# Masked cross attention: the transposing of the row maxima, the projections and the values moved later in the order of steps

## What is computed

```python
q = einsum('oc,bct->bot', Wq, target) + bq      # 256 x 512 for each batch
k = einsum('oc,bcs->bos', Wk, source) + bk
v = einsum('oc,bcs->bos', Wv, source) + bv      # all three: 16 heads of 16 rows
dot = einsum('bhdt,bhds->bhts', q, k) / 4
mask = target_mask[..., None] * source_mask[..., None, :]
dot = mask * dot - (1 - mask) * 1e6
out = einsum('bhts,bhds->bhdt', softmax(dot) * mask, v)
```

## Time and profile before

| what | value |
|---|---|
| median of 3 runs | 3598.25 us |
| the profiled execution | 3600.92 us |
| its span, first to last instruction | 3599.1 us |
| PE busy | 3035.9 us (84%) |
| DVE busy | 1701.8 us (47%) |
| ACT busy | 1241.4 us (34%) |
| POOL busy | 601.1 us (17%) |
| masked cross attention | from 464 us to about 1110 us |

### The profile page before, as it was taken

The page is one execution under the profiler, slowest core; times in us unless marked ns, Lnnn a source line. Parts: engine busy times, 40 slices in busy tenths (PEclk is TensorE's granted clock), DMA queues, the critical chain, the costliest instruction groups (busy, mean ns, idle before and its releaser), DMA issues. The chain is left out here.

```text
span 3599.1 us, 48594 instructions
## 1 busy us (share of the span) xinstructions
PE 3035.9 (84%) x16338; PEld 2037.3 (57%) x16339; DVE 1701.8 (47%) x3232; ACT 1241.4 (34%) x3220; POOL 601.1 (17%) x647
## 2 busy tenths in 40 slices
PE   6999849888881999999788885999999996999894
PEld 4676513333321777777545554888888885444441
DVE  5666646777752111112166663666666664111113
ACT  2333306555660111111044432655655552111110
POOL 1000031232233000000000001333333332300002
PEclk9999959989985999999899997999999998999997
DMA  1000057656734000000100002111211106201323
GB/s 64 19 23 23 13 127 142 147 121 155 142 83 144 12 13 12 13 13 18 44 13 23 23 18 77 48 48 58 83 59 48 41 30 239 108 0 35 128 93 114
DMA packets 127374, 235.40 MB, mean 65 GB/s; under 512 B 15384, under 2 KB 27928, under 8 KB 127216
## 3 DMA queue, kind: packets, MB, share of 16 engines
q1 hardware_dynamic: 106560, 190.20, 18.8%
q0 software_dynamic: 12528, 32.40, 2.7%
q10 hardware_dynamic: 8128, 10.67, 1.0%
HBM read 161.55 MB, written 71.14 MB: 65 GB/s over the span
## 5 line engine op out<-in xcount | busy, mean ns | idle before, releaser
L1295 DVE TENSOR_REDUCE x_minus_max<-banks 128x2 f32<-128x1024 f32 x256 | 308.5, 1223 | 176.4 <-PE banks L1361 174.9
L1243 ACT ACTIVATE x_probs<-banks 128x512 f32<-128x512 f32 x512 | 272.3, 598 | 135.2 <-PE banks L1379 127.5
L481 ACT ACTIVATE a_probs<-banks,a_minus_max 128x128 f32<-128x128 f32 (+1 forms) x512 | 208.6, 425 | 146.5 <-DVE a_minus_max L564 144.8
L1361 PE MATMUL banks<-x_stacked_k,x_stacked_q 51*128 51x512 f32 x512 | 135.6, 480 | 60.4 <-DVE x_whole L1312 21.2
L1379 PE MATMUL banks<-x_stacked_q,x_stacked_k 53*128 53x512 f32 x512 | 162.4, 534 | 22.2 <-ACT x_probs L1243 18.8
L1379 PEld LDWEIGHTS banks<-x_stacked_q,x_stacked_k 53*128 53x128 f32 x512 | 64.6, 203 | 204.4 <-issue 157.5
L2116 POOL TENSOR_TENSOR x_probs<-x_probs,x_inverse 128x512 f32<-128x512 f32 x128 | 133.1, 1040 | 274.6 <-DVE x_inverse L2325 274.6
L2850 DVE TENSOR_TENSOR m_h<-banks,m_silu 128x512 f32<-128x512 f32 x39 | 27.0, 692 | 318.8 <-PE banks L2966 166.3
L2180 ACT ACTIVATE x_probs<-banks,x_minus_max,x_rroot 128x256 f32<-128x256 f32 x256 | 142.9, 566 | 91.4 <-DVE x_minus_max L2291 91.4
L564 DVE TENSOR_REDUCE a_minus_max<-banks 128x2 f32<-128x512 f32 (+1 forms) x192 | 131.8, 687 | 82.4 <-PE banks L714 62.1
L1688 DVE TENSOR_TENSOR f_hT<-banks,f_silu 128x256 f32<-128x256 f32 (+1 forms) x88 | 37.3, 424 | 280.7 <-ACT f_silu L1614 280.7
(11 more groups left out here) (372 smaller groups left out, 7764.6 us busy)
## 6 DMA issues: line engine op xcount, KB each, us to landing
x_parts_dram<-x_parts SPq DMA_DIRECT2D x16, 1024.0 KB, 6.1
x_x<-x_after SPq DMA_DIRECT2D x24, 512.0 KB, 4.3
x_stacked_k<-x_parts_dram SPq DMA_DIRECT2D x96, 128.0 KB
x_stacked_q<-x_parts_dram SPq DMA_DIRECT2D x96, 128.0 KB
x_after<-a_z SPq DMA_DIRECT2D x16, 512.0 KB, 2.8
x_z<-x_after SPq DMA_DIRECT2D x16, 512.0 KB, 7.3
x_heads_dram<-x_heads_out SPq DMA_DIRECT2D x32, 256.0 KB, 4.6
x_after<-x_z SPq DMA_DIRECT2D x16, 512.0 KB, 3.7
```

Of the source, the lines that this page charges most:

```text
L481: ins = act.activation(probs[:, n % 3, i * width:(i + 1) * width], psum[uses.bank(use)][:, i * width:(i + 1) * width], ACT.Exp, bias=minus ...
L1243: act.activation(probs[:, n % 8, :], psum[at.bank(f"exp{n}")], ACT.Exp, scale=SCALE)\
L1295: dve.tensor_reduce(minus_max[:, c % 2, h % 4:h % 4 + 2, t], at.pair(use), AX.X, ALU.max, negate=True)\
```

## The change

`shift` moves from q = 15, 31, 47 and 63 to q = 18, 34, 50 and 66. ACT's copy of its rows is a step of its own now, `copy`, which stands at the same q. `maxima` stays. The projections move from q = 34, 38, 42 and 51 to q = 36, 40, 44 and 53, with their `whole` and `round`, and the second half of the values from q = 19 to q = 23. The first half stays at q = 6. No instruction is added or taken away.

```diff
--- before.py
+++ after.py
@@ -803,10 +803,11 @@
 UNIT_LEAD = 36
 UNITS_IN_TAIL = 1
 MAXIMA_AT = 12
-SHIFT_AT = 15
+SHIFT_AT = 18
+COPY_AT = 18
 SLOTS = 4 * 16
-PIECES_AT = (34, 38, 42, 51)
-VALUES_AT = (6, 19)
+PIECES_AT = (36, 40, 44, 53)
+VALUES_AT = (6, 23)
 FOLD = 32
 HALF = 64
 STACKED_PAIRS = ((0, 0), (0, 1), (1, 0))
@@ -848,7 +849,7 @@
             for kind, at in (("values'", 0), ("more'", 0), ("bias'", 2), ("mask'", 3)):
                 if q == start + at:
                     add((kind, n))
-        for kind, at in (("maxima", MAXIMA_AT), ("shift", SHIFT_AT)):
+        for kind, at in (("maxima", MAXIMA_AT), ("shift", SHIFT_AT), ("copy", COPY_AT)):
             if q in (at, at + 16):
                 add((kind, (q - at) // 16 + 2))
             if q in (at + 32, at + 48):
@@ -1242,10 +1243,9 @@
                         at.wait_full(act, f"exp{n}")
                         act.activation(probs[:, n % 8, :], psum[at.bank(f"exp{n}")], ACT.Exp, scale=SCALE)\
                             .then_inc(free[at.bank(f"exp{n}")], 1)
-                    if kind in ("shift", "shift'"):
-
-                        to = u if kind == "shift" else 1 - u
-                        use = f"{kind}{n}"
+                    if kind in ("copy", "copy'"):
+
+                        use = f"shift{n}" if kind == "copy" else f"shift'{n}"
                         at.wait_full(act, use)
                         act.copy(max_rows[:, n % 2, :], psum[at.bank(use)][0:8, :]).then_inc(free[at.bank(use)], 1)
                         at.wait_free(act, use)
```

## The result

| | before | after |
|---|---|---|
| median | 3599.18 us (3590.18 to 3605.63, 5 runs) | 3617.68 us (3614.4 to 3626.74, 5 runs) |
| the profiled execution | 3600.92 us | 3614.93 us |
| its span | 3599.1 us | 3613.1 us |
| PE's first row of the part that follows | 1120.1 us | 1133.1 us |

The ratio is 1.0051, with a 95% interval of 1.0033 to 1.007: slower, and inside the range. (The median before takes in two runs more than the 3598.25 us of the first table.) Of the 14.0 us between the profiled executions, 13.0 have come by the end of the masked cross attention. On ACT and POOL a line number is now one higher than before (L1244 for L1243, L1175 for L1174).

What follows compares the result with a forecast made beforehand. PE was taken to set the pace, the other engines mostly waiting for it. The terms 23.8 - 20.6 + 3.0 - 9.0 - 5.9 - 3.6 + 3.5 + 21.6 gave +12.8 us, 3611 us against the median of 3598.25; range 3586 to 3634.

Steps and rivals of the forecast that it cites:

- point 6: Later values, ACT's copy, SP's transfers, DMAs of shift 0 and 1: all have slack, so 0.
- point 7: Clock among the new waits of 1.54 us: two falls per batch at 1.8 us, six batches, +21.6 us.
- point 1: Projections two steps later: no context between the two scores, wait 1.54 for 0.55, cycle 6.05 for 5.06, +23.8 us.
- Point 2: Transposing three steps later: five long waits go, -20.6 us; cast still held, so third projection's `whole` late, +3.0 us.
- Point 4: Seam: last transposing and the score behind wait less, -5.9 us; two clock falls fewer, -3.6 us.
- point 3: Clock behind the stall: five falls of 1.8 us go with it, -9.0 us.
- point 5: Transposing at q = 50 takes a bank's turn; score at q = 52 waits some 0.7 in five batches, +3.5 us.
- The fourth rival: Wait moves to `exp 48`, for slower DMAs behind POOL's combine: 1 to 2 us in five batches, about 3618; chance 0.05.
- the pair in the earlier trace: Two PE waits of 0.50 and 0.81 within 2 us, followed by the lower clock; taken as nearest to 1.54.
- the third rival: Clock stays down among waits of 1.54 us: up to 78 us and 3667, half of that 3628; chance 0.10.

Runs made afterwards that it cites:

- run 3: Changed kernel with the projections at q = 38, 42, 46, 55 in place of 36, 40, 44, 53: 3606.69 us, ratio 1.0024 to the kernel before.
- run 4: Changed kernel with `whole` one step behind its projection in place of two: 3593.93 us, ratio 0.9988 to the kernel before.
- run 6: Kernel before with POOL's low parts moved behind the DMAs of the third shift: 3596.36 us, ratio 0.9992.
- run 12: Kernel before with only POOL's DMAs of shift 3 moved ahead of the combine: 3574.37 us, ratio 0.9926.
- run 1: Kernel before with the shifts alone moved, to q = 18, 32, 50, 66: 3607.57 us, ratio 1.0031.
- run 5: Kernel before with only the third shift moved, from q = 47 to 50: 3608.32 us, ratio 1.0029.
- run 8: Kernel before with shifts at q = 15, 31, 50, 66 and `whole` one step behind its projection: 3596.22 us, ratio 0.999.
- run 9: Kernel before with POOL's low parts behind the third shift's DMAs and shift 3's DMAs ahead of the combine: 3588.7 us, ratio 0.9953.
- run 11: Kernel of run 8 with POOL's DMAs of shift 3 also moved ahead of the combine: 3577.26 us, ratio 0.9915 to the kernel before.
- run 7: Changed kernel with the first shift back at q = 15, the rest as changed: 3611.43 us, ratio 1.0031 to the kernel before.
- run 2: Kernel before with the projections alone moved, to q = 36, 40, 44, 53: 3621.19 us, ratio 1.0066.

## Why the prediction was right, and where it wasn't

The total, +12.8 us against the profiled execution, came out at +14.0 (+13.0 at the end of the part); by the medians the change costs 18.5. The range and the sign were right, but two terms were wrong by some 12 us each, point 6 and point 7, and their errors cancel. That the sum came so near is luck.

| step | predicted | measured |
|---|---|---|
| 1 projections | +23.8 | about +24 (a cycle at full clock takes 6.05) |
| 2 long stall | -20.6 | -20.6 |
| 2 what is late behind the cast | +3.0 | +1.4 |
| 4 seam, without clock | -5.9 | about -3 |
| 6 DMAs of the shifts, `exp 32` | 0 | **+12.2** |
| `exp 48` in the seventh batch | in no point | -2.9 |
| 7 clock among the new waits | +21.6 | **about +9** |
| 3, 5 and the clock of 4 | -9.1 | about -6, by difference |

*Point 1* was right, in the form too, but for the split of the wait: 1.26 us of the cycle are waits (0.23 and 1.03) where 0.55 were. The other 0.28 of the 0.99 shows as PE's busy time: two products for the exponentials that ran as one group of 0.49 us run as 0.39 and 0.50, with the wait of 0.23 between them. Of the 24 cycles in batches 0 to 5, 15 took 6.05 to 6.14 us. Runs 3 and 4 take the cost away in two different ways.

*Point 2*: the stall went, the cast of 2.87 us and its end at 737.16 behind POOL's run came as worked out, with the two subtractions and not three. The rest was smaller: only the cycles behind the casts of 2.87 and 3.08 us were longer by it (6.63 and 6.84), for in the other batches (casts of 0.34, 0.45 and 1.26 us) POOL and the cast met otherwise. That POOL can hold the cast for its run and not for one instruction is shown by runs 6 and 12, which changed POOL alone; that any run does it is refuted by run 12. The prediction set this against the Trainium skill ("SBUF — State Buffer", Who interferes with whom), which has the loser blocked for one instruction. Where the low parts follow no DMA issue, the trace agrees with that page: 0.30 us, to the end of one subtraction, at most 1.28 anywhere. Where they do, it disagrees: 2.87 us in the changed kernel, 4.20 in the one before.

*Point 4* saw the transposing's 0.92 and the score's 0.53 go, and missed that with them the context and the exponential behind would wait for ACT (0.37 and 0.98).

*Point 6* is the step that failed: "The DMAs of shift 0 and 1 are issued later, with 14 steps to go: 0". It set no landing time against the 14 steps, and it left out shift 2, for `exp 32`, which moved from q = 15 to 18 and has 14 steps to go as well. In each of batches 0 to 6 these were 1.08 to 2.28 us too short. In the middle batch the DMAs were issued at 706.90 and `exp 32` ran at 716.60, 9.7 us later. The time from issue to landing, first over all of these DMAs, then for the two issued at 706.90:

```profile
DMA to landing us min/median/max: 1.7/2.5/11.5
DMA to landing us min/median/max: 8.9/9.0/9.1
```

Against the median of 2.5 us 14 steps look ample. The long ones are what counts at this place, where the loads of the next batch fill the DMA engines; in the kernel before the same two DMAs took 9.2 us as well, and three steps more hid it. The share of the engines, the column after the clock:

```profile
700.00:717.00 17.00, 15.25 (x81) 5.93 (x80) 12.25 (x13) 11.35 (x22) 1.66 (x3) 0.85 1.08 178
```

From 700 to 717 us it reads 1.08: all of them are busy. The fourth rival had this mechanism, at `exp 48` and at 1 to 2 us in five batches; it was `exp 32` in seven.

*Point 7* had the right mechanism and too large a size. Seven of the 24 cycles ran partly at the lower clock, 7.69 to 8.00 us in place of 6.05, where twelve falls were forecast; that is 12.2 us, and four cycles before the change had lost 3.1 so, which leaves some 9. In the middle batch the waits of 0.97 and 1.03 left the rows behind them at full speed, and the lower level comes behind 1.52 and 0.44 (0.75 for the score at 739.23). But in the first batch it comes behind two cycles with no wait above 0.99:

```profile
585.33 0.50 PE L1361 MATMUL banks<-x_stacked_k,x_stacked_q 51*128 51x512 f32 x2 [0.99 <-DVE x_whole L1312]
585.76 3.63 PE L1402 MATMUL banks<-x_context,x_w_k 128*128 128x512 f32 x4
```

So no length of a single wait, nor the pair in the earlier trace rows, tells where the clock falls. What *point 3* expected back behind the stall is in the remainder: a stretch behind the cast still reads 0.83 (735 to 745), and over the six batches the clock is 0.90 before and after. A batch that stays at the lower level, the third rival, did not come.

The deeper question is why taking 20.6 us of stall away gave nothing back even where point 1 costs nothing (runs 1, 5, 6 and 8: 3596 to 3608 us). Runs 9, 11 and 12 answer it: both the stall and what came to light behind it (the late DMAs for `exp 48`) were made by one thing, DMA issues on POOL that stood behind the combine and ahead of the low parts, not by the place of the transposing. The change moved PE's steps, and left the line that was late. What stays open: how much of the 12.2 us of `exp 32` comes back when they go (run 7), what sets off a fall of the clock, and how points 3, 4 and 5 share the remainder.

## What to carry to other kernels

Before a stall is taken away, look at what arrives during it: here rows lay ready at 707.1 us, and their DMAs were issued at 723.6, behind 16 us in which POOL waited and worked for another batch, and only the stall hid it. Move the ready piece ahead of the one that has to wait; in this case that alone brought 25 us (run 12), where moving the waiting step alone cost 9 (run 5). A slack counted in steps is to be held against the landing times at that place (9 us here) and not against the median of all (2.5), and a wait chain for a bank changes with the remainder of the step number, since that decides what work stands in between.

## What the hardware showed that I had not expected

A cast of 16 columns on DVE, 0.167 us in the median, was held up to 4.7 us beside two or three subtractions on POOL, but only where two DMA issues stood directly ahead of them; without these it was let go with the end of one instruction (at most 1.28). Where the one instruction is longer, so is the hold: two scales of 8x512 at the start of the part took 2.09 and 3.80 us beside four memsets of 3.74 each on POOL, and each ended within 0.05 us of the end of one. A DMA issue without a subtraction behind it held nothing (0.18). The scale of two columns (0.17 us) was held in the same way, for 3.22. Why the issues make that difference no run here shows. Other operations were not held: 26 row maxima read from PSUM, 15 of `whole` and 3 statistics began while such low parts ran, over all the traces, and took at most 1.23, 0.74 and 0.68 us, as elsewhere.

Less waiting did not mean more time at the higher clock: the change and the kernel before have 0.90 over the same stretch, with 67.7 and 66.1 us of waits; run 12, with 57.5, has 0.92, but so has run 2, with 76.3, and run 3, with 59.4, has 0.87.
